# A graph-network kernel: both edge sorts split between one-word scatters and one-hot products, with the source scatters issued in later stages

## What is computed

```
h = relu(layernorm(x));  x = x + L0(h, edges)
h = relu(layernorm(x));  x = x + L1(h, edges)
L0: x_in = gatv2(h; 1); h = relu(batchnorm(x_in @ W1 + b1)); h2 = gatv2(h; 2)
    relu(batchnorm(concat(h2, x_in) @ W2 + b2))
gatv2 (3 heads of 128; N self edges are added):
    xl = h @ Wl + bl; xr = h @ Wr + br
    score = att . leaky_relu(xl[src] + xr[dst]);  alpha = softmax over the edges of one dst
    out = segment_sum(alpha * xl[src], dst) + bias
L1 (8 heads of 16; attention grouped by src):
    q = h[src] @ qTrans; k, v = h[dst] @ kTrans, vTrans
    a = exp(clip(q . k)); out = layernorm(segment_sum(a*v, src) / segment_sum(a, src) + h)
```

## Time and profile before

| what | value |
|---|---|
| median of 3 runs | 6380.7 us (6372.31 to 6382.09) |
| the profiled execution, its own time | 6354.12 us |
| its span in the trace | 6352.2 us |
| busy share of the span: DVE, PE, ACT, POOL | 86%, 78%, 72%, 60% |
| large block of `sort_by_dst` | about 210 to 1525 us |
| `slot_tables` | 1525 to 1568 us |
| `gat_edges` 1 | 1568 to 3195 us |
| node layer 1, batch norm, node tables 2 | 3195 to 3400 us |
| `gat_edges` 2 | 3402 to 5032 us |
| node layer 2, batch norm, residual tables | 5033 to 5205 us |
| `edge_attention` and `finish` | 5210 to 6352 us |

### The profile page before, as it was taken

One profiled execution on the slowest core, in us unless ns is written; L12 is line 12 of the kernel. 1 busy time (PEld: TensorE's weight loads), 2 busy tenths in 40 slices (PEclk: granted clock), 3 DMA queues, 4 the chain that ended last, 5 costly groups with the idle time before them and its releaser, 6 DMA issues. The chain is left out here.

```text
span 6352.2 us, 127992 instructions
## 1 busy us (share of the span) xinstructions
PE 4973.3 (78%) x23046; PEld 2906.5 (46%) x23047; DVE 5465.1 (86%) x13020; ACT 4594.8 (72%) x19630; POOL 3833.8 (60%) x3546
## 2 busy tenths in 40 slices
PE   3797799935888999998878898988889766656663
PEld 2574355512444444444463444444444455555553
DVE  9989988843999999999966999999999866666666
ACT  5576799921999999999926999999999653333332
POOL 0588777784666666666503666666666217777773
PEclk9999999967999999999989999999999977777775
DMA  0262000023555555555604555555555334444444
GB/s 13 58 79 33 2 2 2 2 45 86 147 137 140 139 139 139 139 139 140 123 17 144 139 140 139 140 139 140 141 140 139 67 95 128 130 127 129 127 129 78
DMA packets 352738, 655.93 MB, mean 103 GB/s; under 512 B 110151, under 2 KB 201221, under 8 KB 352116
## 3 DMA queue, kind: packets, MB, share of 16 engines
q0 software_dynamic: 185888, 481.62, 30.1%
q1 hardware_dynamic: 166612, 172.14, 11.0%
HBM read 617.73 MB, written 33.88 MB: 103 GB/s over the span
## 5 line engine op out<-in xcount | busy, mean ns | idle before, releaser
L1268 POOL DMA_INDIRECT feat_area<-xl_table,feat_area x1856 | 1992.5, 1074 | 1499.2 <-PE bank L1342 679.4
L1419 ACT ACTIVATE feat_area<-feat_area 128x130 f32<-128x130 f32 x5568 | 1643.5, 297 | 185.1 <-DVE feat_area L1472 182.6
L1329 PE MATMUL bank<-node_area,feat_area 128*128 x3712 | 1464.8, 518 | 339.6 <-DVE feat_area L1464 176.2
L1403 ACT ACTIVATE feat_area<-feat_area 128x128 f32<-128x128 f32 x4640 | 1442.2, 387 | 31.6 <-issue 31.6
L1342 PE MATMUL bank<-feat_area 128*128 128x390 f32 x3712 | 1405.3, 501 | 34.3 <-ACT feat_area L1403 8.4
L634 POOL DMA_INDIRECT rec_by_dst<-feat_area,gather_col x800 | 979.0, 1224 | 243.7 <-issue 235.5
L1906 POOL DMA_INDIRECT feat_area<-kv_table,gather_src x832 | 808.8, 972 | 467.0 <-issue 252.3
L1329 PEld LDWEIGHTS bank<-node_area,feat_area 128*128 128x128 f32 x3712 | 631.8, 190 | 986.9 <-issue 727.7
L1419 ACT ACTIVATION_READ_ACCUMULATOR feat_area<-feat_area 128x1 f32 x5568 | 1040.3, 187 | 0.0
L1342 PEld LDWEIGHTS bank<-feat_area 128*128 128x128 f32 x3712 | 668.5, 190 | 602.2 <-issue 192.9
L1464 DVE TENSOR_TENSOR feat_area<-bank,feat_area 128x780 f32<-128x780 f32 x928 | 885.9, 955 | 22.3 <-DMA feat_area<-xl_table,feat_area 14.9
(11 more groups left out here) (336 smaller groups left out, 6999.9 us busy)
## 6 DMA issues: line engine op xcount, KB each, us to landing
feat_area<-lo_slot SPq DMA_DIRECT2D x464, 128.0 KB, 3.3
feat_area<-xl_table,feat_area POOLq DMA_INDIRECT x1856, 3.4
feat_area<-lo_slot_src SPq DMA_DIRECT2D x104, 256.0 KB, 3.5
node_area<-lo_edge SPq DMA_DIRECT2D x100, 256.0 KB
xl_table<-feat_area SPq DMA_DIRECT2D x98, 195.0 KB, 2.3
feat_area<-kv_table,gather_src POOLq DMA_INDIRECT x832, 2.8
rec_by_dst<-feat_area,gather_col POOLq DMA_INDIRECT x800
feat_area<-gates SPq DMA_DIRECT2D x348, 32.0 KB
```

The source lines that it names most:

```text
L1268: pool.indirect_dma_start(ring[:, at:at + HE], None, k.xl, bass.IndirectOffsetOnAxis(ap=index[s // CG][:, n:n + 1], axis=0)).then_inc(gath ...
L1329: last = nc.tensor.matmul(pair[s % 2][:, u, 0:HE], pick[s // 2 % 2][:, c:c + P], k.node[:, ds(columns[0], HE)], start=True, stop=True)
L1403: last = nc.scalar.activation(row[:, 0:D], row[:, 0:D], ACT.Copy, scale=row[:, D:D + 1])
L1419: last = nc.scalar.activation(at, at, ACT.Copy, accum_out=score[s // CG][:, to:to + 1])
```

## The change

- A record is **one word**: `node * 256 + lane + 1` (0 is an empty slot), in place of two words in the `dst` route.
- The `dst` table: POOL scatters only the first DST_WRITTEN = 800 - 224 = 576 columns. The last DST_MOVED = 224 go by one-hot products (928 tiles wide, so matmuls of 464 columns); this runs right after the loop that finds the slots, ahead of the search for the `src` slots, which now waits for it on PE (`taken`).
- The `src` table: only the last SRC_MOVED = 200 columns go by products. The first SRC_WRITTEN = 600 are scattered by POOL **later**, by `LateWords.write(pool, n)`, which issues the next n of them: 16 in `slot_tables`, LATE_GAT = 190 spread evenly over the 464 groups of each `gat_edges` (after a group's two gathers), 48 in each `node_layer` and in `node_tables`, the last 60 in `residual_tables`, followed by a wait for all of them.
- A new block `source_tables`, ahead of `edge_attention`, adds the two parts of the `src` table and makes what `permute` made at its end.
- `slot_tables` adds the two parts of the `dst` table; the neighbours across partitions come from two small matmuls in place of two loads of one record per partition; it makes about six more passes over 1024 columns.
- `gat_edges` reads its gather indices straight from `gather_col`: SP's index loads are gone, and POOL's list has no loop.
- The packing of block numbers (`block_row`) is dropped. Key packing adds seven passes over 800 columns and drops two.

Core of the diff:

```
+DST_MOVED = 224
+SRC_MOVED = 200
+DST_WRITTEN = COLS - DST_MOVED
+SRC_WRITTEN = COLS - SRC_MOVED
+LANE_BITS = 10
+LATE_GAT = 190
...
 constants:
-            sp.dma_start(k.rec_d.rearrange("(p s) f -> p (s f)", p=P), fill_d).then_inc(stored, 16)
+            for words in (k.word_d, k.word_s):
+                sp.dma_start(words.rearrange("(p s) f -> p (s f)", p=P), fill).then_inc(stored, 16)
...
 sort_by_dst, ACT:
             pipeline(act, halves, [(1, round_table), (1, keep_rows), (1, mark_earlier)], R)
+            dst_moves.on_scalar(act)
             beside.on_scalar(act, multiplied, halves)
-            move_on_scalar(act)
+            src_moves.on_scalar(act)
...
 PE:
-            beside.on_tensor(pe)
-            move_on_tensor(pe)
+            dst_moves.on_tensor(pe)
+            beside.on_tensor(pe, dst_moves)
+            src_moves.on_tensor(pe)
...
 DVE:
+            dve.wait_ge(ranked, halves)
+            do(nc.vector.memset(k.lo_col[:, T_DST:TILES], 0.0))
+            dst_moves.on_vector(dve, pos_d[:, DST_WRITTEN:], beside.word_dst[:, DST_WRITTEN:], k.lo_col[:, 0:T_DST])
             beside.on_vector(dve)
-            move_on_vector(dve)
+            src_moves.on_vector(dve, beside.pos_i[:, SRC_WRITTEN:], beside.word_src[:, SRC_WRITTEN:], beside.moved_i)
             dve.wait_ge(sorted_src, 1)
...
 Records.write:
-        for c in range(COLS):
+        for c in range(DST_WRITTEN):
...
+class LateWords:
+    def write(self, pool, n):
+        for c in range(self.done, min(self.done + n, SRC_WRITTEN)):
+            turn = c // DEEP
+            if turn:
+                pool.wait_ge(self.written[c % DEEP], 16 * turn)
+                pool.nop(nofuse=True)
+            pool.indirect_dma_start(k.word_s, bass.IndirectOffsetOnAxis(ap=self.slot[:, c:c + 1], axis=0),
+                                    self.word[:, c:c + 1], None).then_inc(self.written[c % DEEP], 16)
+            self.done = c + 1
...
+class Placement:          # the old permute, once for each table, then:
+        for m in range(2):
+            to = slice(m * self.half, (m + 1) * self.half)
+            do(nc.vector.tensor_copy(self.low[:, to], self.out[1][m]))
+            do(nc.vector.scalar_tensor_tensor(out=result[:, to], in0=self.out[0][m], scalar=1024.0, in1=self.low[:, to],
+                                              op0=ALU.mult, op1=ALU.add))
+        dve.sem_inc(self.taken, 1)
...
 gat_edges, POOL:
-                pool.wait_ge(index_set[s // CG], 16 * j + 16)
-            pipeline(pool, groups, [(0, gather)], U)
+            for g in range(groups):
+                s = g % U
+                if g >= U:
+                    pool.wait_ge(summed, g - U + 1)
+                    pool.nop(nofuse=True)
+                for u in range(GS):
+                    ...
+                late.write(pool, (g + 1) * LATE_GAT // groups - g * LATE_GAT // groups)
...
 residual_tables, POOL:
+            late.write(pool, COLS)
+            late.wait(pool)
...
+def source_tables(k):
+            sp.dma_start(written, k.word_s.rearrange("(p t) o -> p (t o)", p=P)[:, 0:T_SRC]).then_inc(loaded, 16)
+            sp.dma_start(moved, k.moved_s).then_inc(loaded, 16)
+            do(nc.vector.tensor_tensor(written, written, moved, ALU.add))
+            do(nc.vector.tensor_scalar(low_i, written, 255, None, ALU.bitwise_and))
+            do(nc.vector.tensor_copy(low_f, low_i))
+            nc.vector.tensor_scalar(k.lo_src[:, :], low_f, -1.0, None, ALU.add).then_inc(lo_set, 1)
+            do(nc.vector.tensor_scalar(k.gather_src[:, :], written, 8, None, ALU.logical_shift_right))
+            (then 7 transposes, 7 copies and 7 stores, as permute had)
```

More of the change, by code:

```diff
@@ L296, in sort_by_dst @@
     one_row, middle_row = cut(P // 2, F16, 1), cut(W // 2, F16, 1)
-    records = Records(k, beside.pay)
+    records = Records(k, beside.word_dst)
     pos_d = records.pos
@@ L337, in _ @@
             do(nc.vector.tensor_copy(lo, part_i))
+            beside.pack(do, beside.word_dst, key["src"], part_i)
             do(nc.vector.tensor_scalar(part_i, key_i, 7, None, ALU.logical_shift_right))
             do(nc.vector.tensor_copy(hi, part_i))
-            beside.key_blocks(do, key["src"])
+            beside.key_blocks(do, key["src"], key["dst"])
         @block.tensor
@@ L876, in slot_tables, with placements, __init__ @@
-def slot_tables(k, rec, block_dram, gathered, key, tag):
+    def placements(self):
+        cut = Carver(self.k.node[:, -2 * T_DST - EC * 4:])
+        return (Placement(self.k, "pd", self.shared, DST_MOVED, T_DST, cut),
+                Placement(self.k, "ps", self.shared, SRC_MOVED, T_SRC, cut))
+class Shared:
+    def __init__(self, iota, cut):
+        n = max(DST_MOVED, SRC_MOVED)
+        self.iota = iota
+        self.part_i, self.lane_f, self.tile_f = cut(n, I32, EC), cut(n, F32, EC), cut(n, F32, EC)
+        self.piece = [cut(n, F32, EC) for _ in range(2)]
+        self.to_tile = [cut(T_DST // 2, F16, EC) for _ in range(MOVE)]
+        self.to_lane = [cut(P, F16, EC) for _ in range(MOVE)]
+        self.at_lane = [cut(P // 2, F16, EC) for _ in range(MOVE)]
+        self.zero = cut(T_DST // 4, F16, EC)
@@ L971, in _ @@
         def _(pe):
+            tiles = k.lo_col[:, :].rearrange("p (t g) -> p g t", g=TG)
+            for half in range(2):
+                for u in range(4):
+                    last = nc.tensor.transpose(k.bank[5 + half][:, u * P:(u + 1) * P], tiles[:, 4 * half + u, :], k.ident[:, :])
+                last.then_inc(words, 1)
+            pe.wait_ge(keys_set, 1)
+            nc.tensor.matmul(k.bank[7][:, 0:1], down, key_f[:, SLOTROW - 1:SLOTROW], start=True, stop=True)
+            nc.tensor.matmul(k.bank[7][:, 1:2], up, key_f[:, 0:1], start=True, stop=True).then_inc(edges, 1)
             pe.wait_ge(rows_ready, 1)
@@ L1197, in table_parts, with node_tables, _ @@
     return on_sync, on_scalar, on_tensor, on_vector
-def node_tables(k, *parts):
+def node_tables(late, k, *parts):
     on_sync, on_scalar, on_tensor, on_vector = table_parts(k, *parts)
     with k.nc.Block() as block:
+        @block.gpsimd
+        def _(pool):
+            late.write(pool, 48)
         block.sync(on_sync)
@@ L1222, in gat_edges @@
     lo_bc = [cut(GS * P, BF16) for _ in range(2)]
-    index = [cut(CT, I32) for _ in range(2)]
     att_w = cut(HE)
@@ L2132, in program @@
         q_area, acc, h = k.node[:, 0:NPAD], k.node[:, NPAD:NPAD + NB * VW], k.node[:, NPAD + NB * VW:2 * NPAD + NB * VW]
[L2133 removed]
+        residual_tables(k, io, scale[:, 0:1], shift[:, 0:1], x_loaded, h, q_area, late)
         k.recycle()
+        source_tables(k)
         edge_attention(k, q_area, acc)
```

405 lines of the change are left out of this document (209 added, 196 removed).

## The result

The changed kernel took **6509.5 us** (median of 4 runs, 6503.84 to 6516.16), the kernel before, beside it, 6381.4 us: a ratio of **1.0203**, 95% interval 1.019 to 1.0216. The forecast was 6155 us, faster; the time lies 235 us above the upper end of the range, on the other side.

The account below looks back on a forecast made before the run. It took PE to bound the products, scatters to slow the tables and DVE to bound the edge stages. Terms -306 + 3 + 20 + 4 + 25 + 13 + 15 = -226 gave 6155 us from 6380.7; range 6100 to 6275.

Parts of the forecast that it names:

- From 282.84, at the rate of the same columns now: Sort block: POOL's dst scatters start at 282.84 and keep their present rate, the 576th issued near 1155.
- I take 1.48 plus a hold of about 0.2: Edge stages: price of each late scatter on POOL, 1.68 us including a hold by DVE.
- POOL then at 3.39 of 3.43: Edge stages: with late scatters POOL needs 3.39 us of a 3.43 us group, so they barely fit.
- the rest, 2.70 us a group: Edge stage of layer 1: the time POOL itself needs in each group, outside its wait for PE.
- 0.733 us a group: Edge stages: POOL's wait for PE, taken as room that allows 1.79 us for each late scatter.
- rival 2: Edge stages: POOL just bounds them, scatters typically 2.05 us each, +99 in all, 6234 us; chance 18%.
- rival 1: Edge stages: held scatters, with displaced gathers held too, make POOL the bound, +346, 6481 us; chance 10%.
- So the scatters slow the tables: Table steps: layer 1's 49 took 130 us beside scatters, layer 2's 73 us where POOL issues nothing.
- node tables +25: `node_tables`: 21 steps beside late scatters at 2.7 us and 28 at 1.49 make 98 us against 73.
- the -48 of layer 1: Layer 1 table steps: only 7 of 49 would still lie beside scatters, 82 us in place of 130.
- Rival 3: Table steps: PE's clock, not scatters, causes the 130 us, so -48 and +25 both go, 6178 us; chance 7%.
- The stated signs: Forecast wrong if the edge stages lose over 60 us each or the sort block ends after 1270.

Follow-up runs that it names:

- with gaps: The changed kernel, still scattering one-word records, with dst slots 8 bytes apart and every second word of the list unused: 6336.6 us.
- with two words: The changed kernel with slots of two words (8 bytes) in the dst list, both written by one scatter: 6349.2 us.
- far edges: The changed kernel with each column's 125 edges taken in groups of five, 4000 edges apart, so a dst scatter's words fall far apart: 6301.2 us.

## Why the prediction was wrong

**The step that failed first**: "From 282.84, at the rate of the same columns now", and with it that `dst` slots cost nothing new. I had listed one-word records as a shorter load and a shorter fill, and never asked what their *writes* do. They put the words of sorted neighbours side by side; +216 us, shown by the kernels with gaps (318 us), with two words (333) and with far edges (322). Alone this turns -226 into -10. No rival had it; the term stood at nothing, without a reason.

**The second**: "I take 1.48 plus a hold of about 0.2", and with it "POOL then at 3.39 of 3.43". POOL needed 3.68 us a group, and the two stages lost 230 us in place of 20. The scatter's own price, 1.60 us, lay under the 1.68 taken. Two other terms were wrong. The gathers' part of "the rest, 2.70 us a group" was held constant, but displaced gathers took 1.207 us in place of 1.083, 0.25 us a group or 0.60 for each scatter: 2.20 in all. And "0.733 us a group" of room counts pauses of 0.30 us as waits: by the earlier trace rows, (518.4 - 816 x 0.30)/408 = 0.67 us were free, 1.63 us for each scatter and not 1.79. With these, (2.20 - 1.63) x 380 = +217 us, near the 230 measured. So rival 2 had the mechanism, that POOL just bounds the stages, but with its typical price of 2.05 against 1.79 only +99; rival 1 had named the displaced gathers.

**Third**, "So the scatters slow the tables": right for the kernel before, wrongly carried over to all scatters. The steps go from 129.5 to 83.1 us when the `dst` scatters beside them spread their words; with source scatters beside them they take 73. Hence node tables +25 came out as nothing (73.8 us against 72.9 in layer 2), and the -48 of layer 1 as -57, by an accident of the late loop. Rival 3 (the clock does it) falls too: an edit that moves only the scatters' words brings 83.1 us at the same place, and the clock rises with it.

**Right**: the products (-251 of -258), their two means per column, `slot_tables`, POOL's last `dst` scatter (1151.6, near 1155), the residual block ended by POOL and the source tables (the row of both, with node layer 2, +28 of +30 us). With the loop mended by far edges the norm begins at 1047.4, forecast 1046; there is luck in that, a loop 9 us shorter and a start 5 us later than it assumed. The stated signs were there: the edge stages lost over 60 us each and the block's end lay beyond 1270.

"DMA: Bandwidth & Descriptors" (Specifications) of the Trainium skill says that a transfer under 512 B is done as read-modify-write. It covers both record sizes alike, so by it alone nothing would have changed between them; the runs show that it matters where such writes fall beside each other. The rule might have made me ask, and I had not used it.

## What to carry to other kernels

When a record written by an indirect DMA shrinks, look at where the words of one instruction fall, not only at the bytes saved: sorted keys make neighbours of them, and spacing or interleaving costs little. An engine with room on average has none for free: charge an inserted issue for what it does to the issues behind it, take the fixed pause before each issue out of the waits before calling them room, and try a half dose as well as the full one. Before moving work to a place "beside" other work, ask which property of it (order, target, size) did the harm in the place where harm was seen.

## What the hardware showed that I had not expected

- 125 four-byte writes side by side raised the engine time a packet of loads from another list (nine packets in ten have 2048 bytes) from 0.146 us (8 bytes apart) to 0.450; the longest such packet took 10.9 us, 5.7 with gaps. PE, which waited in that loop, was granted 0.72 on average, between its two levels of 1.2 and 2.4 GHz, and 0.98 with gaps.
- Source scatters, to random slots, beside the stores of the tables: no cost (73.1 against 72.5 us). `dst` scatters to neighbouring slots: 57 us (129.5 against 72.5); with spread words 11 to 19 us (83.1 and 91.8), with gaps of a word 23 (95.7).
- A gather's issue on POOL took 0.95 us or up to 3.48 by where it met DVE: its mean rose from 1.083 to 1.207 us when POOL's issues no longer waited for PE.
- A scatter's issue on POOL took 0.94 us for 8 words and 1.26 for 125, in the same stage.
